# A graph kernel with two more gathered tiles and two fewer dense ones per hop, dense steps dealt over more slots, and a fourth buffer of node values

## The reference

```
h = relu(layernorm(x))
# layer 0: a message per edge, weights by edge type, summed at the destination
msg = where(type == 0, h[src] @ W_data.T + b_data, h[src] @ W_control.T + b_control)
x = x + relu(segment_sum(msg, dst) + h @ W_self.T + b_self)
# layer 1: two hops over the same edges
h = relu(layernorm(x));  norm = rsqrt(deg)[src] * rsqrt(deg)[dst]
y1 = segment_sum(h[src] * norm, dst);  y2 = segment_sum(y1[src] * norm, dst)
x = x + (h + y1 + y2) / 3
```

## Time and profile before

| what | value |
|---|---|
| median of 3 runs | 3672.07 us (3669.55 to 3674.48) |
| profiled execution | 3670.85 us, its span 3668.8 us |
| mean granted TensorE clock | 0.906 |
| busy PE / ACT / POOL / DVE | 3144.8 / 2652.7 / 2472.8 / 1793.7 us |
| dense matmuls, L1491 | 12544 |
| chunks gathered, L1114 | 1333 in stage 0, 1162 in the hops |
| casts of counts, L1283 | 896 |

### The profile page before, as it was taken

How to read it: one execution, slowest core, us unless ns; L and a number is a source line. 1 busy time by engine, 2 the same in 40 slices (tenths; PEclk the granted TensorE clock), 3 DMA queues, 4 the chain that set the end, 5 groups by cost and what they waited for, 6 DMA issues and landing times.

```text
span 3668.8 us, 64228 instructions
## 1 busy us (share of the span) xinstructions
PE 3144.8 (86%) x23900; PEld 2855.9 (78%) x23900; DVE 1793.7 (49%) x4171; ACT 2652.7 (72%) x2875; POOL 2472.8 (67%) x2610
## 2 busy tenths in 40 slices
PE   5578788888888867667667999999997999999998
PEld 3368677777677755445457999999997999999998
DVE  6864655554545578888883232333333222222223
ACT  3366666776667654554546889999995899999997
POOL 2477667777777777777774666666664766666666
PEclk8889899998899976776768999999998999999999
DMA  8623333333333375555556788888889878887876
GB/s 241 177 84 91 97 94 102 113 87 112 100 85 112 105 230 183 184 187 183 189 182 208 228 242 247 240 251 241 253 252 317 245 230 233 235 235 233 235 233 199
DMA packets 444207, 687.74 MB, mean 187 GB/s; under 512 B 62390, under 2 KB 373569, under 8 KB 435699
## 3 DMA queue, kind: packets, MB, share of 16 engines
q1 hardware_dynamic: 343827, 441.27, 37.6%
q0 software_dynamic: 99200, 241.92, 23.8%
q10 hardware_dynamic: 864, 0.39, 0.1%
HBM read 511.64 MB, written 171.70 MB: 186 GB/s over the span
## 4 chain that ended last, share of the span: by engine, by line
PE 45%; DVE 3%; ACT 1%; issue 1%; DMA 1%; POOL 0%; DVEq 0%; SPq 0%; POOLq 0%; ACTq 0%
PE wide L1491 39%; PE sums_bank L1367 3%; PE sums_bank L1365 1%; ACT strip_ring L1283 1%; PE wide L1403 1%; DVE flat L1900 1%; DVE flat L1897 1%; DMA stage<-strips 1%; POOL rows L1114 0%; DVE xin L1754 0%; DMA hop_table<-stage 0%; DVE scaled L1756 0%; DVE scaled L1746 0%; ACT scaled L1194 0%; DVE stage L1898 0%
## 5 line engine op out<-in xcount | busy, mean ns | idle before, releaser
L1114 POOL DMA_INDIRECT flat<-typed_table,index x1333 | 1297.8, 974 | 464.6 <-issue 400.6
L1283 ACT CAST strip_ring<-stage 128x1792 fp32r<-128x1792 uint8 x896 | 1495.0, 1687 | 144.9 <-PE wide L1491 126.3
L1491 PE MATMUL wide<-table_parts,strip_ring 128*128 128x256 f32 x12544 | 1542.6, 285 | 38.7 <-ACT strip_ring L1283 31.5
L1491 PEld LDWEIGHTS wide<-table_parts,strip_ring 128*128 128x128 f32 x12544 | 1528.0, 194 | 42.6 <-issue 25.7
L1114 POOL DMA_INDIRECT rows<-hop_table,index x1162 | 1111.6, 957 | 608.5 <-issue 314.4
L1265 ACT CAST stage<-wide 128x392 uint16<-128x392 f32 x1344 | 547.2, 517 | 464.6 <-PE wide L1403 463.6
L1403 PE MATMUL wide<-stage,flat 128*128 128x196 bf16 x2688 | 445.8, 286 | 301.1 <-DVE flat L1900 164.3
L1403 PEld LDWEIGHTS wide<-stage,flat 128*128 128x128 bf16 x2688 | 211.7, 108 | 517.6 <-DVE flat L1900 202.4
L1417 PE MATMUL turned_bank<-typed_ring,table_parts 128*128 128x256 f32 x3920 | 538.3, 298 | 76.8 <-ACT typed_ring L1276 70.4
L1845 DVE SCALAR_TENSOR_TENSOR sums<-sums_bank,in_upper,sums 128x128 f32 (+1 forms) x459 | 160.4, 350 | 876.8 <-PE sums_bank L1367 674.5
L1417 PEld LDWEIGHTS turned_bank<-typed_ring,table_parts 128*128 128x128 f32 x3920 | 509.2, 203 | 96.5 <-issue 59.4
(11 more groups left out here) (183 smaller groups left out, 1400.3 us busy)
## 6 DMA issues: line engine op xcount, KB each, us to landing
stage<-strips SPq DMA_DIRECT2D x896, 224.0 KB, 3.7
strips<-stage SPq DMA_DIRECT2D x64, 1568.0 KB
table_parts<-hop_table SPq DMA_DIRECT2D x28, 896.0 KB, 9.7
flat<-typed_table,index POOLq DMA_INDIRECT x1333
rows<-hop_table,index POOLq DMA_INDIRECT x1162
resid<-xin SPq DMA_DIRECT2D x50, 256.0 KB, 3.7
xin<-resid SPq DMA_DIRECT2D x50, 256.0 KB, 4.9
typed_table<-flat SPq DMA_DIRECT2D x49, 256.0 KB, 2.4
```

Of the source, the lines that this page charges most:

```text
L1114: pool.indirect_dma_start(out=gathered(k, o % RING, c), out_offset=None, in_=tables[k], in_offset=bass.IndirectOffsetOnAxis(ap=index[:, ch ...
L1283: act.copy(strip_ring[:, number % STRIP_RING], counts_ring[place]).then_inc(strip_cast, 1)
L1491: last = pe.matmul(wide[:, nth % 4, 0:PARTS * P], strip_ring[:, number % STRIP_RING, b - first, :], table_parts[:, b, :, :].rearrange("p n ...
```

## The change

Four edits.

1. **62 dense tiles instead of 64.** The sixteenth batch (number 15, `MIXED`) is split: tiles 60 and 61 dense, 62 and 63 gathered. Hops begin five groups earlier: 78 slots, 434 steps. The gathered part of batch 15 is closed in slot 6 and copied aside (`later_part`, in words of `index` that are not read in a hop) until the batch is finished. Stage 0 builds 62 strips: 496 quads instead of 512, over the same slots.
2. **Steps over all but two slots.** `dense_slots` is 76 of 78, where it was 69 of 73.
3. **Lead steps** are dealt 3, 1, 2, 4, 4, 4 over the six empty slots instead of 3 each. A reload after hop 1 may start one slot later than before.
4. **A fourth buffer** of node values in the hops, also in words of `index`; and **the copy of the high part** in hop 1 is made by DVE instead of ACT. In stage 0 it stays with ACT.

```diff
-DENSE_TILES = DENSE_BATCHES * NODE_BLOCKS
+DENSE_TILES = 62
+MIXED = DENSE_BATCHES - 1
+MIXED_DENSE = DENSE_TILES - MIXED * NODE_BLOCKS
-DENSE_SLOTS = 69
+SLOTS_BEHIND_DENSE = 2
-LEAD_AT_ONCE = 3
+LEAD_AT = (3, 1, 2, 4, 4, 4)
+HOP_XIN = 4
...
+    dense_slots = hop_groups - SLOTS_BEHIND_DENSE
...
-        return lead_steps[k] + min(rest, -(-(i + 1) * rest // DENSE_SLOTS))
+        return lead_steps[k] + min(rest, -(-(i + 1) * rest // dense_slots))
...
-    events += [spread_out(hop_wanted(k), XIN) for k in range(1, HOPS + 1)]
+    events += [spread_out(hop_wanted(k), HOP_XIN) for k in range(1, HOPS + 1)]
...
+        def xin_of(n, general):
+            if xin_place[n] < XIN:
+                return xin[:, xin_place[n], :]
+            if general:
+                return flat[:, row_words - BATCH:row_words]
+            return index[:, 0:BATCH].bitcast(F32)
...
             if k:
-                return slot_of_step(1, last_step_with(piece))
+                return slot_of_step(1, last_step_with(piece)) + 1
...
(ACT)
-                        if finishing and k < HOPS:
+                        if finishing and k == 0:
                             finish(finishing[0], k, finishing[1], False)
...
(DVE, finish)
+                    if not general and s == MIXED:
+                        dve.wait_ge(cut_made, next(first_cut[k] + j for j, (_, cut_batch) in enumerate(cuts[k]) if cut_batch == s) + 1)
+                        dve.tensor_tensor(in_blocks(values, blocks)[:, MIXED_DENSE:blocks], later_part,
+                                          over_features(factors[:, MIXED_DENSE:blocks], blocks - MIXED_DENSE), ALU.mult)
...
                 dve.wait_ge(scaled_ready, n + 1)
+                if k:
+                    dve.tensor_copy(high_of(n, k, s, general), in_blocks(values, blocks)).then_inc(high_ready, 1)
                 dve.wait_ge(high_ready, n + 1)
...
(DVE, cut)
+                    if k and s == MIXED:
+                        if k > 1:
+                            dve.wait_ge(fresh_made, event_of[k - 1][MIXED] + 1)
+                        dve.tensor_copy(later_part, sums[:, kept, MIXED_DENSE:NODE_BLOCKS, 0:P])
```

More of the change, by code:

```diff
@@ L211, in hop_wanted @@
     def hop_wanted(k):
-        dense = [(tile_slot[k][(s + 1) * NODE_BLOCKS - 1], s) for s in range(DENSE_BATCHES)]
+        dense = [(tile_slot[k][min((s + 1) * NODE_BLOCKS, DENSE_TILES) - 1], s) for s in range(DENSE_BATCHES)]
         return dense + [(slot, s) for slot, s in cuts[k] if s >= DENSE_BATCHES]
@@ L623, in scaled_of @@
             return scaled[:, 0 if k == 0 else n % 2, :]
-        xin_place = [n % FIRST_XIN if n < total else n % XIN for n in range(events_all)]
+        xin_place = [n % FIRST_XIN if n < total else n % HOP_XIN for n in range(events_all)]
+        def xin_of(n, general):
[4 more added lines that the diff above has]
+            return index[:, 0:BATCH].bitcast(F32)
+        assert BATCH <= first_group * CHUNKS
         def xin_uses(n):
@@ L697, in steps_at @@
             if i >= slots_of(k) and k < HOPS:
-                first = (i - slots_of(k)) * LEAD_AT_ONCE
-                return [step_number(k + 1, j) for j in range(first, min(first + LEAD_AT_ONCE, lead_steps[k + 1]))]
+                first = sum(LEAD_AT[:i - slots_of(k)])
+                return [step_number(k + 1, j) for j in range(first, min(first + LEAD_AT[i - slots_of(k)], lead_steps[k + 1]))]
             if 0 < k and i < hop_groups:
@@ L802, in reloads_of_slot @@
             return [piece for slot, piece in reload_orders[k] if slot == i]
-        assert all(lead_steps[k] <= LEAD_AT_ONCE * LAST for k in range(1, HOPS + 1))
+        assert len(LEAD_AT) == LAST and all(lead_steps[k] <= sum(LEAD_AT) for k in range(1, HOPS + 1))
         def edge_round(i):
@@ L895, in _, with load_nodes @@
                          pair_tile.rearrange("p (k e) n -> p k (e n)", k=PAIR_TILES)).then_inc(pairs_stored, 16)
-            def load_nodes(n, k, s, before):
+            def load_nodes(n, k, s, before, general):
                 place = xin_place[n]
@@ L913, in load_nodes @@
                     sp.wait_ge(resid_stored[xin_place[before]], 16 * xin_uses(before))
-                    sp.dma_start(in_blocks(xin[:, place, :]), of_batch(resid, s)).then_inc(xin_in[place], 16)
+                    sp.dma_start(in_blocks(xin_of(n, general)), of_batch(resid, s)).then_inc(xin_in[place], 16)
             def load_own(s, place, landed):
@@ L1252, in _ @@
                         act.copy(ring_index[:, :], index[:, ds(g * CHUNKS, CHUNKS)]).then_inc(rest_index, 1)
-                    for s in range(total):
-                        finish(k * total + s, k, s, True)
+                    if k == 0:
+                        for s in range(total):
+                            finish(s, k, s, True)
                 act.nop()
@@ L1696, in take_degrees @@
                 dve.tensor_scalar(linked_now, degree, 0.0, None, ALU.is_gt)
-                dve.tensor_scalar(spread_now[:, 1, :], degree, 1.0, None, ALU.max).then_inc(degree_read if s >= TYPED_BATCHES else typed_degree, 1)
+                read = dve.tensor_scalar(spread_now[:, 1, :], degree, 1.0, None, ALU.max)
+                if s >= TYPED_BATCHES:
+                    read.then_inc(degree_read, 1)
             def finish(n, k, s, source, read, general):
@@ L1703, in finish @@
                 columns = blocks * P
-                nodes_in = xin[:, xin_place[n], 0:columns]
+                nodes_in = xin_of(n, general)[:, 0:columns]
                 factors = inv[:, s * NODE_BLOCKS:s * NODE_BLOCKS + blocks]
```

25 lines of the change are left out of this document (14 added, 11 removed).

## The result

The changed kernel takes 3609.06 us (median of 4 runs, 3606.64 to 3615.20) against 3670.81 of the kernel before beside it: ratio 0.9834, 95% interval 0.9823 to 0.9846. The forecast was 3608 us with a range of 3586 to 3638. The profiled execution took 3611.11 us, its span is 3609.0; before they were 3670.85 and 3668.8.

What follows compares the result with a forecast made beforehand. No engine was at its limit in stage 0 and TensorE bound both hops; -27.1 - 16.7 - 7.7 - 1.5 - 4.2 - 6 = -63.2 us from 3670.85 gave 3608 us, range 3586 to 3638.

Steps and rivals of the forecast that it cites:

- (a): Both hops: 14 dense steps out and 5 groups in, -18.7 us a hop, -37.4 for two, booked by stretches.
- (b): Hop 1, slot 1 to end of dense: 797.0 to 769.9 us, -27.1; ACT's 12.0 loss goes, 11 at reloads stays.
- (c): Hop 2, slot 0 to end of dense: 794.2 to 777.5 us, -16.7.
- (d): Into hop 1: root behind four casts, not six, 6 us, and one step fewer in slot 0, 1.7; together -7.7 us.
- (e): Between the hops: one TensorE restart, step 7 at T+30.3 (T: end of hop 1's dense slots); gain 1.5 us, ends +8, -8.
- (f): The tail after hop 2's dense work: no wait for rows, 17.2 us down to about 13, -4.2.
- (g): Stage 0: 16 fewer quads over the same 162 slots, POOL setting the pace; -6 us, ends -18 and +4.
- The danger: Both hops: POOL, 10.1 us a group, is level with TensorE's slots and binds from 10.34 us a group on.
- A: Rival, less gain: the joints pay back through reloads, handover, stage 0 and (d); 3636 us, chance 0.19.
- B: Rival, more gain: stage 0 gives 18 us, reloads lose only 5, handover -8; 3584 us, chance 0.10.
- C: Rival, slower: POOL becomes the bound of both hops; 3633 us at 10.5 a group, 3708 at 11.0; chance 0.06.
- D: Rival: ACT's casts still hold TensorE in hop 1, the 12 us stay, 3620 us; chance within the main 0.65.

Runs made afterwards that it cites:

- e5_before_dve_copy: The kernel before, with only the copy of the high part in the hops moved from ACT to DVE: 3659.15 us, ratio 0.9964.
- e6_counts_by_slot: The changed kernel, with SP starting count loads ahead of a hop slot by slot, not all behind the last store: 3593.34 us, ratio 0.9788.
- e7_both: The changed kernel with count loads handed out by slot and at most two reloads started in a slot instead of three: 3587.49 us, ratio 0.9775.
- e8_between: The changed kernel with count loads by slot, three reloads a slot, and in a hop's last slots counts between the reloads: 3588.49 us, ratio 0.9778.

## Why the prediction was right, step by step

(a), (b) and (c), the hops. The unit prices held (9.33 and 11.01 us a slot), the loss of 12.0 us in hop 1 vanished, and both hops came within 0.7 us of the forecast. The 64-tile run gives the work of two tiles as 18.9 us a hop in hop 2 against 18.7. The 11 us kept for the last slots were 12.2. Their reason, bytes at 340 GB/s, holds for the stretch as a whole: from slot 71 to T the changed kernel moved 319 GB/s and the variants with other orders 325 to 333, and under SP's new order dealing the reloads in another way changed the stretch from slot 71 to slot 0 of hop 2 by 0.5 us at most (107.0 to 107.5), the store ahead of them by 1.9. How much is lost ahead of T goes by the dealing: at 62 tiles 9.9 to 13.9 us with three reloads in a slot, 5.2 to 6.5 with two. And behind T the changed kernel moved only 281 GB/s, where SP's new order had 322: there it was not bytes alone.

(d), into hop 1: -4.9 instead of -7.7. The step that was mis-sized is "the last reload follows the lead casts" with 4.60 us taken on unchanged. The root did move, from 9.4 to 5.0 us after the first dense step (ACT's line), and the gap at the restart did go to 0.70. But the end of the stretch hangs on the last reload (SP's line, of the kernel before; the changed kernel's stands above at 1976.70):

```profile
1950.00 0.20 ACT L1250 ACTIVATE batch_spread<-batch_spread 128x8 f32<-128x8 f32 x1
```

```profile
1989.81 0.37 SPq L1007 DMA_DIRECT2D table_parts<-hop_table  x1
```

It was issued 38.1 us after the first dense step before, took 7.9 to land, and slot 1 came 13.4 behind that: 59.4. After, these are 31.7, 10.6 and 12.2: 54.5. So the reload gained 6.4 us, but landed 2.7 us more slowly, and the wait in slot 0 grew to 7.22. I had seen the reload behind 18 loads of counts and taken that as given. It was worth 9.5 us, more than the whole term.

(e), the handover: +0.9 instead of -1.5, inside its own ends. The order of events is the forecast one (six lead steps, then idle, one restart), the restart 2.7 us later, T + 33.0 for T + 30.3: the third finish waited 2.46 us for a store that took 7.51 us beside the reloads, and the counts landed 6.65 us after issue behind two of them. The prediction opens this part with ACT's copies; with them gone alone (`e5_before_dve_copy`) the handover stayed at 49.3 us.

(f): -5.3 for -4.2, since no wait for rows is left. (g): -6.7 for -6 is luck in part. Over the profiled executions with 62 tiles the first dense step stands at 1941.7 on the mean (8 kernels) and with 64 at 1952.9 (3), with 60 at 1926.3 (1): 11 us, then 15, for two tiles each. By these means the term was sized at half, and the pair of executions in the table happens to show 6.7 only. That TensorE's work stands in stage 0's path for more than POOL's waits of 63.4 us say is the likely reason; no run shows it.

POOL. The danger was read rightly: level at 10.1 us, no harm at 62 tiles, the bound at 60. DVE's new copy did cost POOL something: 21 of POOL's operations overlap one of the new casts and take 1.09 us on the mean instead of 0.95. POOL's rows and DVE's:

```profile
2074.43 0.95 POOL L1128 DMA_INDIRECT rows<-hop_table,index  x1 [0.31 <-issue]
2075.68 1.08 POOL L1128 DMA_INDIRECT rows<-hop_table,index  x1 [0.30 <-issue]
```

```profile
2075.97 0.43 DVE L1783 CAST stage<-scaled 128x512 fp32r<-128x512 f32 x1
```

That is 3 us in all where 12 were allowed for. The 12 came from one operation of 1.42 us, and DVE also had a memset of 0.49 us beside it, from 2411.60, which the prediction doesn't count. The Trainium skill, "SBUF — State Buffer", "SBUF: two separate sides", has an operation stand until the copy ends, with an example of five times the duration. This trace shows 0.13 us more on the mean beside a copy of 0.43, and 0.27 at most. In five of the variants two operations of 1.38 to 1.46 us stand beside a cast, but beside DVE's other finish operations too; the cast's share in them isn't shown.

The rivals. A (the joints pay back) had two of its four parts in small: (d) and (e) brought 5.2 us less than forecast. B's reload gain exists ahead of T but is lost again behind it for the most part. Its 18 us from stage 0 did not come. C starts at 60 tiles. D is out: with DVE's copy the casts don't hold TensorE, which is busy for all of 300 us in mid-hop while ACT is busy for 272 of them.

## What to carry to other kernels

Price a stretch by TensorE's own unit times and look at what remains: here nothing was lost for 70 slots, and what was still to be won lay in the joints of the parts. There, read the issuing queue as a program of its own: loads that wait for casts, put ahead of a transfer that could have gone at once, cost 17 us, while the order of the lead steps moved the time by nothing that shows. And when two engines have been brought level, try the next notch at once; it tells where the bound lies better than any sum.

## What the hardware showed beyond the forecast

- A wait of TensorE can cost more than its length: 7.22 us of it cost 9.46, as the 84 matmuls behind it took 12.30 us at a granted clock of 0.81, and not 10.22 at 1.00.
- Dealing the reloads in another way did not help where the queues were full: 327, 326 and 333 GB/s in the windows from slot 71 to T in `e6_counts_by_slot`, `e7_both` and `e8_between`, and the same end of the stretch, 107.0 to 107.5 us on.
- SP itself is held there: three reloads took it 6.11 us to issue behind T in `e7_both`, where one takes 0.37 us at 1976.70.
- The first dense step moved by 10 us (1937.8 to 1948.0) between eight kernels with the same work in stage 0, on two chips. A part worth under 5 us there can't be shown by one profiled execution.
